# Last attention of a four-layer program: the maxima of four banks in one operation, the subtraction per tile, and the small operations between them regrouped

## The reference

```python
# _L2_ffn_ref, the end: the two chosen experts of each token, weighted
mixed_output = jnp.sum(topk_expert_outputs * topk_weights[..., None], axis=2)
# _L3_xattn_ref: 16 heads of 8, 64 keys
attn = jnp.einsum('bhqc,bhkc->bhqk', qh, kh) * SCALE
attn = jax.nn.softmax(attn, axis=-1)
out = jnp.einsum('bhqk,bhkc->bhqc', attn, vh)
out = out @ o_w.T + o_b
# _L3_ffn_ref: routing of the next part, two experts of 8
logits = xf @ router_w.T + experts_bias
rw, sel = jax.lax.top_k(logits, K)
...
x = x + _L2_ffn_ref(_layernorm(x, axis=-1), ...)
x = x + _L3_xattn_ref(_layernorm(x, axis=-1), ctx_1024, ctx_1024, ...)
x = x + _L3_ffn_ref(_layernorm(x, axis=-1), ...)
```

## Time and profile before

| | us |
|---|---|
| three runs | 1619.09, 1623.52, 1630.98 (median 1623.52) |
| profiled execution | 1622.06 |
| its span | 1620.3 |
| busy in the span: TensorE, VectorE, ScalarE, GpSimd | 1347.2, 1011.2, 886.9, 591.5 |

### The profile page before, as it was taken

One profiled execution on the slowest core, in us unless ns is written; L12 is line 12 of the kernel. 1 busy time (PEld: TensorE's weight loads), 2 busy tenths in 40 slices (PEclk: granted clock), 3 DMA queues, 4 the chain that ended last, 5 costly groups with the idle time before them and its releaser, 6 DMA issues. The chain is left out here.

```text
span 1620.3 us, 43124 instructions
## 1 busy us (share of the span) xinstructions
PE 1347.2 (83%) x16879; PEld 1137.8 (70%) x16887; DVE 1011.2 (62%) x2666; ACT 886.9 (55%) x2048; POOL 591.5 (37%) x569
## 2 busy tenths in 40 slices
PE   7999999899999989934899659995177888778883
PEld 6889999867888958832466449994066666678883
DVE  8798897644443359977568674553377777533335
ACT  5666666534454559974466245662155545326664
POOL 3433433400000024324677226654523333434552
PEclk9999999999999999976799879997587778879997
DMA  6411100099990023200000102222101100012225
GB/s 189 176 34 32 33 18 3 6 146 148 154 100 1 1 61 115 89 1 14 14 19 12 54 15 70 71 64 56 42 24 31 31 28 22 30 50 62 71 66 172
DMA packets 148823, 94.10 MB, mean 58 GB/s; under 512 B 56240, under 2 KB 136624, under 8 KB 148112
## 3 DMA queue, kind: packets, MB, share of 16 engines
q1 hardware_dynamic: 139984, 73.51, 22.7%
q0 software_dynamic: 8640, 17.84, 3.7%
HBM read 51.32 MB, written 39.99 MB: 56 GB/s over the span
## 5 line engine op out<-in xcount | busy, mean ns | idle before, releaser
L1737 POOL DMA_INDIRECT moe_x_rows<-moe_rows,moe_source x71 | 87.8, 1237 | 90.4 <-DVE moe_source L1829 51.6
L439 POOL TENSOR_TENSOR wide_probs<-wide_probs,wide_key_mask 128x512 f32<-128x512 f32 x44 | 65.7, 1513 | 117.4 <-ACT wide_probs L623 117.4
L2444 DVE TENSOR_TENSOR moe_hidden<-banks,moe_gate 128x256 f32<-128x256 f32 x103 | 43.1, 423 | 103.5 <-ACT moe_gate L2663 79.8
L2252 POOL DMA_INDIRECT moe_results<-moe_y_rows,moe_until_blocks x71 | 68.8, 968 | 88.6 <-DVE moe_y_rows L2456 69.7
L919 POOL TENSOR_TENSOR attn_col_bd<-attn_col_t,group_mask_sb 128x1024 f32<-128x1024 f32 x32 | 60.6, 1894 | 106.1 <-ACT attn_row_t L1134 106.1
L889 POOL MEMSET attn_v_bd<- 128x576 f32 x2 | 1.2, 614 | 250.9 <-POOLq L168 250.9
L2663 ACT ACTIVATE moe_gate<-banks 128x256 f32<-128x256 f32 x103 | 39.8, 393 | 90.3 <-PE banks L2887 79.0
L2057 POOL DMA_INDIRECT moe_rows<-moe_xhat,moe_slot x64 | 62.2, 972 | 73.3 <-DVE moe_slot L2380 54.3
L1009 DVE TENSOR_REDUCE attn_top<-banks 128x32 f32<-128x2048 f32 x32 | 73.1, 2284 | 22.9 <-PE banks L1204 22.9
L2207 POOL DMA_INDIRECT moe_until_blocks<-moe_results,moe_slot x64 | 61.7, 963 | 43.5 <-POOLq L168 25.4
L2887 PE MATMUL banks<-moe_xb_t,moe_until_blocks 128*128 128x128 f32 x568 | 77.0, 279 | 0.0
(11 more groups left out here) (461 smaller groups left out, 4394.0 us busy)
## 6 DMA issues: line engine op xcount, KB each, us to landing
moe_rows<-route_empty_sb SPq DMA_DIRECT2D x8, 2624.0 KB, 26.1
attn_ctx<-in_ctx_t SPq DMA_DIRECT2D x48, 128.0 KB, 2.4
moe_until_blocks<-moe_rows SPq DMA_DIRECT2D x71, 66.0 KB
moe_pack_sb<-in_moe_pack SPq DMA_DIRECT2D x8, 578.0 KB, 4.0
moe_results<-moe_y_rows SPq DMA_DIRECT2D x71, 64.0 KB, 1.5
moe_w_sb<-in_moe_w SPq DMA_DIRECT2D x2, 2048.0 KB, 7.2
moe_until_back<-moe_results SPq DMA_DIRECT2D x16, 256.0 KB, 6.1
moe_pack_sb<-in_moe_pack SPq DMA_DIRECT2D x9, 384.0 KB, 4.5
```

The source lines that it names most:

```text
L439: nc.gpsimd.tensor_tensor(some, some, keys, ALU.mult).then_inc(masked, 1)
L1737: nc.gpsimd.indirect_dma_start(x_rows[b % GATHERS][:], None, rows, bass.IndirectOffsetOnAxis(ap=source[:, b:b + 1], axis=0)).then_inc(gath ...
L2252: nc.gpsimd.indirect_dma_start(results, bass.IndirectOffsetOnAxis(ap=x_rows[b % LOADS][:, P:P + 1].bitcast(U32), axis=0), y_rows[b % GATHE ...
```

## The change

The four maxima of a step become one reduction over the four banks (128x2048), and the four subtractions two, one per tile (128x1024 each); each of these counts `shifted` up, so the transposes of the first tile's probabilities need only the first. The small operations that stood between them are put ahead of the reduction (five pieces of choice, norm and chain) and behind the subtractions. The subtractions come directly behind the addition into x. The parts of the gathered results are cut differently: duo 3 is a part of its own, added in step 2 with its chain, and duos 4 and 5 are added in step 3 instead of step 2, with their chain in the same step. GpSimd issues the gathers of three duos before the clears, and of five after.

```diff
 BACK_AHEAD = 8
-BACK_PARTS = [range(0, 1), range(1, 2), range(2, 4), range(4, 6), range(6, 8), range(8, 12), range(12, 16)]
-BACK_AT = {2: [4, 5], 4: [6, 7], 5: [8], 6: [9, 10], 7: [11], 8: [12], 9: [13], 10: [14], 11: [15]}
-BACK_LINKS = {3: 3, 5: 4, 7: 5, 11: 6}
+BACK_PARTS = [range(0, 1), range(1, 2), range(2, 3), range(3, 4), range(4, 6), range(6, 8), range(8, 12), range(12, 16)]
+BACK_AT = {2: [3], 3: [4, 5], 4: [6, 7], 5: [8], 6: [9, 10], 7: [11], 8: [12], 9: [13], 10: [14], 11: [15]}
...
-                for duo in range(BACK_AHEAD // 2):
+                for duo in range(3):
                     bring_back(duo)
...
-                for duo in range(BACK_AHEAD // 2, BACK_AHEAD):
+                for duo in range(3, BACK_AHEAD):
                     bring_back(duo)
...
-                def tops(u, banks):
-                    for j in banks:
-                        if j == 0:
-                            dve.wait_ge(scored, u + 1)
-                        nc.vector.tensor_reduce(top[:, j], s_bank[j][:].rearrange("p (n k) -> p n k", k=SEQ), AX, ALU.max
-                                                ).then_inc(topped, 1)
-
-                def shift_down(u, j):
-                    if j == 0 and u >= 2:
+                def tops(u):
+                    dve.wait_ge(scored, u + 1)
+                    nc.vector.tensor_reduce(top[:].rearrange("p j n -> p (j n)"), core.banks[:, 0:4 * 512].rearrange("p (n k) -> p n k", k=SEQ),
+                                            AX, ALU.max).then_inc(topped, 1)
+
+                def shift_down(u):
+                    if u >= 2:
                         dve.wait_ge(pt_made, 4 * u - 4)
-                    dve.wait_ge(topped, 4 * u + 1 + j)
-                    ins = nc.vector.tensor_tensor(
-                        probs[u % 2][:, :, 4 * j:4 * j + 4], s_bank[j][:].rearrange("p (t g k) -> p t g k", t=2, k=SEQ),
-                        top[:, j].rearrange("p (t g) -> p t g", t=2).unsqueeze(3).to_broadcast([P, 2, 4, SEQ]), ALU.subtract)
-                    if j == 3:
-                        ins.then_inc(shifted, 1)
+                    dve.wait_ge(topped, u + 1)
+                    for t in range(2):
+                        scored_part = core.banks[:, 0:4 * 512].rearrange("p (j t g k) -> p t j g k", j=4, t=2, k=SEQ)[:, t]
+                        nc.vector.tensor_tensor(
+                            probs[u % 2][:, t].rearrange("p (j g) k -> p j g k", j=4), scored_part,
+                            top[:].rearrange("p j (t g) -> p t j g", t=2)[:, t].unsqueeze(3).to_broadcast([P, 4, 4, SEQ]),
+                            ALU.subtract).then_inc(shifted, 1)
 
                 def multiply(m):
...
                     if s >= 10 and s % 2 == 0:
                         place((s - 10) // 2)
-                    choose_parts(choosing, 0, 1)
-                    norm_parts(spilled, 7, 9)
+                    for n in range(5):
+                        choose_parts(choosing, n, n + 1)
+                        norm_parts(spilled, 7 + n, 8 + n)
+                        some_links(to_back, 1)
                     if inside(b):
-                        tops(b, (0,))
-                    some_links(to_back, 3)
-                    choose_parts(choosing, 1, 3)
-                    norm_parts(spilled, 9, 11)
-                    if inside(b):
-                        tops(b, (1,))
-                    some_links(to_back, 3)
-                    choose_parts(choosing, 3, 5)
-                    norm_parts(spilled, 11, 13)
+                        tops(b)
                     if s == STEPS_ALL - 1:
                         multiply(0)
                         multiply(1)
...
                                                 ALU.add).then_inc(added, 1)
-                        choose_parts(choosing, 5, 6)
-                        norm_parts(spilled, 13, 14)
+                    if inside(b):
+                        shift_down(b)
+                    if inside(f):
                         dve.wait_ge(added, f + 1)
                         nc.vector.bn_stats(core.stats[:, 2 * f], core.x[:, 2 * f])
                         nc.vector.bn_stats(core.stats[:, 2 * f + 1], core.x[:, 2 * f + 1]).then_inc(duo_stats_made, 1)
...
-                    else:
-                        choose_parts(choosing, 5, 6)
-                        norm_parts(spilled, 13, 14)
-                    choose_parts(choosing, 6, 7)
-                    norm_parts(spilled, 14, 15)
-                    if inside(b):
-                        tops(b, (2,))
-                    some_links(to_back, 3)
                     for duo in duos:
                         add_back(duo, 0)
-                    choose_parts(choosing, 7, 9)
-                    norm_parts(spilled, 15, NORM_PARTS)
-                    norm_parts(norming, 0, 1)
-                    if inside(b):
-                        tops(b, (3,))
-                    some_links(to_back, 3)
+                    choose_parts(choosing, 5, 6)
+                    norm_parts(spilled, 12, 13)
                     for duo in duos:
                         add_back(duo, 1)
-                    choose_parts(choosing, 9, 11)
-                    norm_parts(norming, 1, 2)
-                    for j in range(4):
-                        if inside(b):
-                            shift_down(b, j)
-                        if j == 0:
-                            choose_parts(choosing, 11, 12)
-                            for duo in duos:
-                                stats_back(duo)
-                            if s in BACK_LINKS and duos:
-                                to_back = links_back(BACK_LINKS[s])
-                        else:
-                            some_links(to_back, 4)
-                        if j < 3:
-                            norm_parts(norming, 2 + j, 3 + j)
+                    choose_parts(choosing, 6, 7)
+                    norm_parts(spilled, 13, 14)
+                    for duo in duos:
+                        stats_back(duo)
+                    if s in BACK_LINKS and duos:
+                        to_back = links_back(BACK_LINKS[s])
+                    norm_parts(spilled, 14, NORM_PARTS)
+                    for n in range(7):
+                        choose_parts(choosing, 7 + n, min(8 + n, CHOOSE_PARTS))
+                        norm_parts(norming, n, n + 1)
+                        some_links(to_back, 2)
                     if s in BACK_LINKS:
                         some_links(to_back, NORM_LINKS)
                         shifts(tiles_back(BACK_LINKS[s]))
-                    norm_parts(norming, 5, 7)
                     if choosing in range(QUADS):
                         tally(choosing)
...
-                        pe.wait_ge(shifted, u)
+                        pe.wait_ge(shifted, 2 * u)
...
                 def probs_back(u, t):
-                    pe.wait_ge(shifted, u + 1)
+                    pe.wait_ge(shifted, 2 * u + 1 + t)
...
                     if s == STEPS_ALL - 2:
-                        pe.wait_ge(shifted, DUOS)
+                        pe.wait_ge(shifted, 2 * DUOS)
```

1 line of the change is left out of this document (added).

## The result

| | kernel before | kernel after |
|---|---|---|
| median of 13 runs | 1623.52 us (1617.04 to 1630.98) | 1613.11 us (1601.30 to 1619.06) |
| ratio, 95% interval | | 0.9941 (0.9921 to 0.9962) |
| span of the profiled execution | 1620.3 us | 1609.4 us |

The change made the kernel 0.6% faster, 6 to 13 us. The forecast was +3 us and no measurable change. Two further comparisons gave 0.998 (0.9942 to 1.0017) and 0.9942 (0.9916 to 0.9969); the three, weighted by their intervals, give 0.995 +- 0.0015, so 6 to 11 us.

What follows compares the result with a forecast made beforehand. In most steps TensorE and ScalarE were taken to be late, with room on VectorE. Terms 0 + 0 + 3.0 - 1.5 + 1.5 = +3.0 took 1622.06 to about 1625 us, range 1603 to 1635.

Steps and rivals of the forecast that it cites:

- The early stretch: Before step 3: TensorE's 30 us wait still ends with the last gather, at 1162.7; taken as 0, bounds 0 to -25.
- Rival C: Early stall: if it hangs on gather and clear order or VectorE's additions, about -19 us, 1603; chance 0.11.
- The additions moved: Steps 3 to 4: duos 4 and 5 added in step 3 make TensorE's transposes of the heads late, +3.0 us.
- Big operations: VectorE's maxima and subtractions in 16 steps: 0.31 us saved a step, 5.0 in all, covered, so 0 in the sum.
- Step 11 to 12: Near 1300 us: scores no longer wait for the last subtraction and the heads come earlier, -1.5 us.
- the addition behind the long reduction: Addition into x comes later behind one reduction in steps at the upper clock, delaying TensorE's first attend, +1.5 us.
- rival D: Addition into x: if y is early in slow steps too, each addition comes 1.2 us later, 19 us more, 1641; chance 0.08.
- Rival B: Ten steps, 1195 to 1341: shorter VectorE chain keeps the clock at its upper level, 20 us less, 1602; chance 0.12.

Runs made afterwards that it cites:

- v_only2: Second run of the kernel after with old parts and 16 and 16 gathers: first addition 69.2 us behind the first gather, next 15 steps 202.0 us.
- a_gather16: The kernel after with GpSimd's gathers 16 and 16 as before: ratio 1.0019 to the kernel before.
- a_oldtables: The kernel after with the kernel before's three lines of tables (parts of the gathered results): ratios 0.9934 and 0.9921 to the kernel before.

## Why the prediction was wrong

- **The early stretch, taken as 0: the step that failed.** The reading that the wait ends with the last gather holds for before and after (not for v_only2, where it ended 7 us ahead of it), and "the burst's end does not move" was right. The conclusion was not. It took the 30 us for one wait, whose end is all that counts; but during the series engines advance, slowly or in pauses, and what has got through by its end is off the path afterwards. With the clears at 1125 instead of 1130, step 2's norm, projections, maxima and subtractions are done by 1147. That is worth 6.5 us (76.3 to 69.8) on the kernel before; with the new steps 16 and 16 gave 76.1, 69.2 and 74.1 and 12 and 20 gave 69.6 and 69.9, so there the mean gain is 3.4. The times bear the order out: a_gather16 has 1.0019 +- 0.0035 where the kernel after has 0.995 +- 0.0015. Rival C named the order of the gathers and clears as a possible cause, with -19 us at 0.11: right place, size three times too large, since it let the stall vanish.
- **The additions moved, +3.0.** Measured +3.9 (69.7 to 73.6), in all three traces of after. Right in sign and mechanism: VectorE is last, and TensorE waits 1.88 us and on. It was worked out for a step that begins at 1175.87; it begins 7 us earlier and costs the same. One reading in it was wrong: TensorE's L2785 did not wait for the heads before. Its row has no wait in front, and it starts 0.12 us behind them.
- **Big operations, 0.31 a step.** Confirmed, 0.26 to 0.31. The rule of the Trainium skill on the drain points to 0.85 ("VectorE: DVE Perf Modes", The DRAIN you can't avoid); neither the old nor the new rows show such a gap between instructions in a row. The same section adds that a next operation that is not held starts earlier, which fits these rows; the prediction left this out.
- **Step 11 to 12, -1.5, and the addition behind the long reduction, +1.5.** The waits of TensorE's scores for the subtraction are gone, as forecast. The addition waits less for TensorE (7.7 us instead of 15.0), so the reduction has used up the margin, as rival D feared, but no more than that; step 8 of the kernel after has no idle time between them:

```profile
1237.99 2.29 DVE L2425 TENSOR_REDUCE attn_top<-banks 128x32 f32<-128x2048 f32 x1 [0.77 <-PE banks L2755]
...
1240.20 0.41 DVE L2503 TENSOR_TENSOR x<-banks,attn_based 128x256 f32<-128x256 f32 x1
```

  D's +19 did not come. The two terms are below what a trace can tell, since 15 steps of one kernel scatter by 2 to 6 us.
- **Rival B.** Steps at a higher clock do exist with the new order (197.5 to 202 us), but in the kernel after the 15 steps took 206 to 211 against 208 to 214: no gain there that shows.

The time did stay within 1% of before, as forecast, but on the other side: the missed term is larger than the +3.0 that was seen. The sum by the measured terms is -6.5 + 3.9 = -2.6 us up to the first addition. The times say 6 to 11 us less. The traces from the first gather to the sixteenth addition (280.8, 279.6 and 284.3 for after, 286.0 and 283.7 for before) say -3.3, with a scatter of 3 each. What stands between is open. So is why the second half of the steps, the same code in both, took 100.7 and 101.7 us in a_oldtables and 104.6, 107.8 and 106.9 in the three traces of after.

## What to carry to other kernels

A wait that ends with somebody's burst is not one block: ask which work could get through inside it, and where its pauses stand against what is ready then; moving a pause forward by 5 us was worth 6.5 us, and moving it by one duo more cost 9. A part of a change can be a loss that the sum hides: take the parts apart before keeping all of them (here the old tables with the rest were 0.992 to 0.993, the whole 0.995). And compare stages only over several traces: one execution had 9 us of chance in a stage that nobody had touched.

## What was not expected of the hardware

While GpSimd issues a long series of gathers by index (40 in the early stretch), 1.25 us apart, TensorE, ScalarE and VectorE issue single instructions 0.7 to 2.8 us apart or none at all, with no semaphore to wait for that the profile shows; 52 gathers replaced by plain transfers of SyncE took 40 us off the time of the kernel after. The number of bytes is the same in both. The hold doesn't begin with the series: in the kernel before VectorE's links of duo 0 run without a gap from 1118.13 to 1121.46, 8 to 11 us into it, and the first of duo 1's that is late stands 2.30 us until 1126.96, 17 us into it. By what path GpSimd holds them was not found out.
